# Left-over channels of two projections as half-height matmuls in alternating rows

## What is computed

```python
Qs = (msa[:, :, 0] @ Wq_s) * scale_s              # query of row 0, per column
sw = softmax(Qs @ Ks)                             # over the 128 rows, Ks = msa @ Wk_s
Q = (x @ Wq) * scaling * sw
K = x @ Wk
V = x @ Wv
QK = einsum('brihd,brjhd->bhij', Q, K)            # 192 x 192 per head, summed over rows
out = einsum('bhij,brjhd->brihd', softmax(QK), V)
x = x + out
```

## Time and profile before

| | us |
|---|---|
| three runs | 669.31, 673.8, 676.18 |
| median | 673.8 |
| span of the profiled execution | 670.4 |
| TensorE matmul busy | 521.5 |
| TensorE weight loads busy (beside matmuls) | 427.5 |
| VectorE busy | 436.3 |
| ScalarE busy | 253.9 |
| GpSimd busy | 225.4 |

### The profile page before, as it was taken

How to read it: one execution, slowest core, us unless ns; L and a number is a source line. 1 busy time by engine, 2 the same in 40 slices (tenths; PEclk the granted TensorE clock), 3 DMA queues, 4 the chain that set the end, 5 groups by cost and what they waited for, 6 DMA issues and landing times.

```text
span 670.4 us, 14214 instructions
## 1 busy us (share of the span) xinstructions
PE 521.5 (78%) x4984; PEld 427.5 (64%) x4984; DVE 436.3 (65%) x981; ACT 253.9 (38%) x555; POOL 225.4 (34%) x231
## 2 busy tenths in 40 slices
PE   0040499997279999999989999999799999157771
PEld 0030288987246666666659999999799888146561
DVE  3999757899726666666664668777556794224453
ACT  0030255786135565556550216555311233022221
POOL 1010123688013333333330005665400084134444
PEclk9995565998579999999999999999899999587887
DMA  8991015789937677777856006777379999999997
GB/s 285 421 427 68 0 48 142 221 237 250 241 107 267 225 246 245 228 265 222 259 153 225 1 15 221 236 237 235 122 251 336 315 315 321 313 315 293 307 285 216
DMA packets 122265, 152.81 MB, mean 228 GB/s; under 512 B 21552, under 2 KB 107120, under 8 KB 120432
## 3 DMA queue, kind: packets, MB, share of 16 engines
q1 hardware_dynamic: 119968, 151.01, 71.3%
q10 hardware_dynamic: 2256, 1.23, 0.7%
HBM read 95.60 MB, written 56.62 MB: 227 GB/s over the span
## 4 chain that ended last, share of the span: by engine, by line
PE 61%; SPq 12%; DVE 11%; DMA 9%; POOL 2%; issue 2%; ACTq 1%; ACT 1%; POOLq 0%; DVEq 0%
DMA BIG<-in_x 7%; PE PS L978 7%; PE PS L979 7%; PE PS L980 7%; PE PS L981 7%; PE PS L982 7%; DVE EXTRA L591 6%; PE PS L1010 4%; PE PS L860 3%; PE PS L1039 3%; PE PS L1040 2%; PE PS L1043 2%; PE PS L1041 2%; PE PS L1042 2%; SPq L422 2%; SPq L397 2%
## 5 line engine op out<-in xcount | busy, mean ns | idle before, releaser
L457 POOL TENSOR_TENSOR BIG<-EXTRA,BIG 128x192 f32 (+1 forms) x144 | 106.5, 740 | 208.5 <-ACT BIG L529 208.3
L758 DVE TENSOR_TENSOR EXTRA<-PS,SW 128x192 f32<-128x192 f32 (+1 forms) x144 | 73.4, 510 | 81.7 <-ACT BIG L542 81.7
L978 PE MATMUL PS<-WP,EXTRA 128*128 128x384 f16 (+1 forms) x384 | 110.4, 288 | 14.2 <-DMA EXTRA<-xt_scratch 12.9
L979 PE MATMUL PS<-WP,EXTRA 128*128 128x384 f16 (+1 forms) x384 | 110.4, 288 | 0.0
L980 PE MATMUL PS<-WP,EXTRA 128*128 128x384 f16 (+1 forms) x384 | 110.4, 288 | 0.0
L981 PE MATMUL PS<-WP,EXTRA 128*128 128x384 f16 (+1 forms) x384 | 110.3, 287 | 0.0
L982 PE MATMUL PS<-WP,EXTRA 128*128 128x384 f16 (+1 forms) x384 | 110.2, 287 | 0.0
L827 DVE SCALAR_TENSOR_TENSOR BIG<-PS,small,BIG 128x512 f32<-128x512 f32 x96 | 64.5, 736 | 60.5 <-DMA BIG<-in_x 57.4
L467 POOL TENSOR_TENSOR BIG<-BIG,EXTRA 64x512 f32<-64x512 f32 x48 | 60.3, 1256 | 119.7 <-DVE BIG L827 62.6
L1010 PE MATMUL PS<-BIG,EXTRA 128*128 128x256 f16 x576 | 69.4, 286 | 31.7 <-DVE BIG L827 31.7
L1010 PEld LDWEIGHTS PS<-BIG,EXTRA 128*128 128x128 f16 x576 | 58.8, 103 | 42.0 <-DVE BIG L827 32.8
(11 more groups left out here) (157 smaller groups left out, 958.2 us busy)
## 6 DMA issues: line engine op xcount, KB each, us to landing
EXTRA<-xt_scratch SPq DMA_DIRECT2D x48, 512.0 KB, 3.6
BIG<-in_x SPq DMA_DIRECT2D x6, 3072.0 KB, 20.9
v_scratch<-EXTRA SPq DMA_DIRECT2D x48, 384.0 KB, 3.8
EXTRA<-xt_scratch SPq DMA_DIRECT2D x48, 256.0 KB, 3.8
BIG<-in_x SPq DMA_DIRECT2D x8, 1536.0 KB, 13.1
out_x<-BIG SPq DMA_DIRECT2D x8, 1536.0 KB, 12.8
BIG<-v_scratch SPq DMA_DIRECT2D x6, 1536.0 KB, 10.9
xt_scratch<-BIG SPq DMA_DIRECT2D x12, 512.0 KB, 3.3
```

The lines of the kernel that those rows point to most:

```text
L457: pool.tensor_tensor(QA[:, :, bass.ds(SI[h] * n + low, SI[h])], TQ[h][g % 4], QA[:, :, bass.ds(SI[h] * n, SI[h])], ALU.subtract).then_inc( ...
L758: v.tensor_tensor(TQ[h][g % 4].rearrange("p (m d) i -> p m d i", d=D), ps[:, :, 0:EH].rearrange("p i (m d) -> p m d i", d=D), swv.unsqueez ...
L978: mm(po, xh0, WP[:, 0, 0, wc], start=True, stop=False)
L979: mm(po, xh0, WP[:, 1, 0, wc], start=False, stop=False)
```

## The change

The left-over 64 channels are stored as pairs of columns: an even column in rows 0 to 63 and the odd column next to it in rows 64 to 127, highs and lows in different slots. A pair of columns is then projected by six matmuls of 128 rows (three for each column, as before) and six of 64 rows (x highs with weight highs, x highs with weight lows, x lows with weight highs; for the even column in the upper rows, then for the odd one in the lower rows, in turn). The product of x lows with weight lows, which L982 included, is no longer made. The stores to DRAM go from seven to five DMAs for two chunks. For h = 1 the two columns of a pair lie in different PSUM banks, so KA is read with one more dimension (ScalarE and VectorE), and q's multiplication is made in two instructions of two columns.

```diff
-        STORES = 16 * 7
+        STORES = 16 * 5
...
-            return ps if h == 0 else ps.rearrange("p a (b n) -> p (a b) n", b=2)
+            return ps if h == 0 else ps.rearrange("p a (b n) -> p b a n", b=2)
...
-                for s in range(2):
-                    to = rest[s * E1:(s + 1) * E1]
-                    sp.dma_start(to[:, :, 0, :], mixed[0:E1, s::2, :]).then_inc(stored, 16)
-                    sp.dma_start(to[:, :, 1, :], odd[E1:P, s::2, :]).then_inc(stored, 16)
+                sp.dma_start(rest[0:E1], mixed[0:E1]).then_inc(stored, 16)
+                sp.dma_start(rest[E1:P], odd[E1:P]).then_inc(stored, 16)
...
-                        nc.scalar.copy(KA[:, :, bass.ds(SI[h] * n, SI[h])],
-                                       ps[:, :, EH:2 * EH].rearrange("p i m -> p m i")).then_inc(s_kvh[h], 1)
+                        if h == 0:
...
+                        else:
+                            nc.scalar.copy(KA[:, :, bass.ds(SI[h] * n, SI[h])].rearrange("p m (b a) -> p m b a", a=2),
+                                           ps[:, :, :, EH:2 * EH].rearrange("p b a m -> p m b a")
+                                           ).then_inc(s_kvh[h], 1)
...
-                        v.tensor_tensor(TQ[h][g % 4].rearrange("p (m d) i -> p m d i", d=D),
-                                        ps[:, :, 0:EH].rearrange("p i (m d) -> p m d i", d=D),
-                                        swv.unsqueeze(2).to_broadcast([P, HALF, D, si]),
-                                        ALU.mult).then_inc(s_tq[h], 1)
+                        tq = TQ[h][g % 4].rearrange("p (m d) i -> p m d i", d=D)
+                        for i in range(0, si, 2):
+                            pq = ps[:, :, 0:EH] if h == 0 else ps[:, i // 2, :, 0:EH]
+                            ins = v.tensor_tensor(tq[:, :, :, i:i + 2], pq.rearrange("p i (m d) -> p m d i", d=D),
+                                                  swv[:, :, i:i + 2].unsqueeze(2).to_broadcast([P, HALF, D, 2]),
+                                                  ALU.mult)
+                        ins.then_inc(s_tq[h], 1)
...
-                    for i in range(SI[h]):
-                        il = at + i
-                        po = ps[:, i, 0:CW[h]]
-                        slot = (il % 2) * (CI // 2) + il // 2
-                        xh0 = XT[b][:, slot * R:(slot + 1) * R]
-                        xl0 = XT[b][:, (CI + slot) * R:(CI + slot + 1) * R]
-                        x1 = XT[b][:, (2 * CI + slot) * R:(2 * CI + slot + 1) * R]
-                        mm(po, xh0, WP[:, 0, 0, wc], start=True, stop=False)
-                        mm(po, xh0, WP[:, 1, 0, wc], start=False, stop=False)
-                        mm(po, xl0, WP[:, 0, 0, wc], start=False, stop=False)
-                        mm(po, x1, WP[:, 0, 1, wc], start=False, stop=False)
-                        ins = mm(po, x1, WP[:, 1, 1, wc], start=False, stop=True)
+                    for even in range(0, SI[h], 2):
+                        outs = [ps[:, i, 0:CW[h]] if h == 0 else ps[:, even // 2, i, 0:CW[h]] for i in range(2)]
+                        for i in range(2):
+                            il = at + even + i
+                            po = outs[i]
+                            slot = (il % 2) * (CI // 2) + il // 2
+                            xh0 = XT[b][:, slot * R:(slot + 1) * R]
+                            xl0 = XT[b][:, (CI + slot) * R:(CI + slot + 1) * R]
+                            mm(po, xh0, WP[:, 0, 0, wc], start=even == 0, stop=False, skip_group_check=True)
+                            mm(po, xh0, WP[:, 1, 0, wc], start=False, stop=False, skip_group_check=True)
+                            mm(po, xl0, WP[:, 0, 0, wc], start=False, stop=False, skip_group_check=True)
+
+                        for s, w in ((0, 0), (0, 1), (1, 0)):
+                            for i, rows in ((0, slice(0, E1)), (1, slice(E1, P))):
+                                o = (2 * CI + s * (CI // 2) + (at + even) // 2) * R
+                                ins = mm(outs[i], XT[b][rows, o:o + R], WP[rows, w, 1, wc],
+                                         start=False, stop=s == 1, skip_group_check=True)
```

More of the change, by code:

```diff
@@ L320, in _ @@
                 full = xt_dram[c // 2, :, 0:4 * CI * R].rearrange("p (c a n) -> p c a n", a=2, n=512)
-                rest = xt_dram[c // 2, :, 4 * CI * R:6 * CI * R].rearrange("p (c a n) -> p c a n", a=2, n=512)
+                rest = xt_dram[c // 2, :, 4 * CI * R:6 * CI * R].rearrange("p (c n) -> p c n", n=512)
                 src = BIG[:, c * CI * E:(c + 2) * CI * E].bitcast(fp16)
@@ L541, in body @@
                                            ps[:, :, 2 * EH:2 * EH + E]).then_inc(s_kvh[h], 1)
-                        nc.scalar.copy(KA[:, :, bass.ds(SI[h] * n, SI[h])],
-                                       ps[:, :, EH:2 * EH].rearrange("p i m -> p m i")).then_inc(s_kvh[h], 1)
+                        if h == 0:
+                            nc.scalar.copy(KA[:, :, bass.ds(SI[h] * n, SI[h])],
+                                           ps[:, :, EH:2 * EH].rearrange("p i m -> p m i")).then_inc(s_kvh[h], 1)
+                        else:
+                            nc.scalar.copy(KA[:, :, bass.ds(SI[h] * n, SI[h])].rearrange("p m (b a) -> p m b a", a=2),
+                                           ps[:, :, :, EH:2 * EH].rearrange("p b a m -> p m b a")
+                                           ).then_inc(s_kvh[h], 1)
                         if g or not isinstance(t, int):
@@ L765, in body @@
                                             ALU.subtract)
-                        v.tensor_tensor(KA[:, :, bass.ds(si * n + C, si)],
-                                        ps[:, :, EH:2 * EH].rearrange("p i m -> p m i"),
-                                        KA[:, :, bass.ds(si * n, si)], ALU.subtract).then_inc(s_kvl[h], 1)
+                        kl, kh = (KA[:, :, bass.ds(si * n + o, si)] for o in (C, 0))
+                        if h == 0:
+                            pk = ps[:, :, EH:2 * EH].rearrange("p i m -> p m i")
+                        else:
+                            pk = ps[:, :, :, EH:2 * EH].rearrange("p b a m -> p m b a")
+                            kl, kh = (q.rearrange("p m (b a) -> p m b a", a=2) for q in (kl, kh))
+                        v.tensor_tensor(kl, pk, kh, ALU.subtract).then_inc(s_kvl[h], 1)
                 body(0)
```

## The result

The changed kernel takes 686.15 us (683.09 to 686.99, 4 runs) against 674.99 us of the kernel before (669.31 to 677.97, 4 runs): a ratio of 1.018 (95% interval 1.012 to 1.023). The forecast was 688.8 us, 15.0 us over the kernel before; it came out 11.2 us over.

The account below looks back on a forecast made before the run. TensorE was taken to bound the projections, with SP's stores setting their start. Span 670.4 + 20.0 (matmuls and switches) − 5 (stores) = 685.4 us; the median, 673.8 + 15.0, gives 688.8 us, range 664 to 722.

Parts of the forecast that it names:

- The bound: Projection stages: TensorE is busy all the time, so time added to a step's TensorE work shows in full.
- The overlap: Projection matmuls: upper and lower halves run together, six taking the time of three; 23.5 us back in all.
- The stagger: Half-height matmuls: the second of an upper and lower pair needs its own weights first, 17 ns once a pair.
- The change of height: Projection steps: each switch between 128 and 64 rows costs 105 ns (90 + 15), two switches a pair.
- The sum of the two: Both projection halves, switches and stagger less the saved matmul: +6.1 us and +13.9 us, +20.0 us together.
- The stores: SP's queue before the projections: five DMAs for seven, 5.8 to 6.0 us a pair of chunks, saving 5 us.
- VectorE at nothing: Projection steps: split q multiplication and reordered KA reads cost nothing, hidden behind the TensorE step.
- A: Rival at the projection matmuls: no overlap, halves run one after the other, 67.4 us more, 756 us; chance 0.14.
- B: Rival at the height switches: the switch is free, its drain hidden, so the kernel is faster, 648.5 us; chance 0.13.
- C: Rival at the stores: the whole 12.9 us wait before the projections goes, 680.9 us; chance 0.11.
- the break-even: Height switches in the projections: below 66 ns a switch the change wins.
- the 15 ns between an upper and a lower start: Sign in the projection timeline: an upper and a lower matmul start some 15 ns apart.

Follow-up runs that it names:

- run 3: Changed kernel with three full-height matmuls in place of a pair's six half-height ones, so no change of height (products not the reference's): 644.53 us, ratio 0.958.
- run 8: Kernel before with only q's second-half multiplication split into two instructions of 192 elements: 675.18 us against 673.44, ratio 1.0039.
- run 6: Changed kernel with all six half-height matmuls of a pair in rows 0 to 63: 845.36 us.
- run 1: Changed kernel with a pair's half-height matmuls ordered three upper, then three lower, instead of in turn: 687.08 us, ratio 1.024 to the kernel before.

## Why the prediction was right

**The bound.** TensorE sets the step, and no other engine or transfer took over, down to 1.46 and 0.74 us a pair (run 3). Shown.

**The overlap.** Forecast at its full bound, and it is there; the gain of one matmul a pair is real. The stagger was booked at 17 ns and is within 4: a pair takes 1.675 and 0.955 us where the forecast's terms give 1.69 and 0.97. The Trainium skill's 4 ns ("TensorE: Matmul & The Clock Gate", Part 3) fits the trace: two together span 0.34 us where one spans 0.33.

**The change of height.** Forecast 105 ns, from fp32 rows; measured 106 to 107 ns in fp16, in four kernels with changes against the one without. Its two pieces hold too, 0.09 us of pause and 0.01 to 0.02 us for the exposed load. This is the term that made the sign of the result, and it could be read from four transposes of the kernel before. The Trainium skill, "TensorEngine Tiling (Array Packing)", Key Properties, says that a change of the tiling mode drains TensorE. The trace agrees for fp16 now as well, with 0.09 us of pause.

**The sum of the two.** +20.0 us forecast; by the measured periods 96 x (0.050 + 0.130) = 17.3 us. The difference is nearly all the stagger, 2 x 96 x 13 ns = 2.5 us. In the two profiles the projection stages grew by 3.8 + 12.2 = 16.0 us; the 1.3 us between that and the periods, in the first half above all, are not accounted for.

**The stores.** 5 us forecast, with 5.8 to 6.0 us a pair of chunks; measured 5.8 us a pair, and a start 5.3 us earlier by the means of twelve profiles. That the transfers then set the pace fits the DMA share of 0.95; no run varied the bytes. The later landing of the reload was not in my sum, and the shorter run of the stores made up for it: that the two cancel is luck. In the changed kernel's own profile the start moved by 2.8 us only. Its third pair of stores began at 120.33 us in place of 118.35, which is spread: with five stores that point lies anywhere between 117.9 and 120.4.

**VectorE at nothing.** Right, if the 0.4% of run 8 is no effect. The reordered reads of KA had no run of their own, but run 3 has them, and the split too, and its pair takes nine matmul times.

**Rivals.** A was ruled out by the timeline, and run 6 made it on purpose: it costs 159 us over the changed kernel, over twice the 67 that I gave it: I had given a fall of the clock no more than the tail of this rival, and it made some 90 of the 159 us. B (a free change) is out: 106 ns, not under 66. But the break-even that it rested on was the useful number, since it says what a better order has to reach. C is out: 7.9 of the 12.9 us wait are still there, and no profile starts the projections before 181.4 us.

**Wrong steps beside it.** Of what was to show the forecast, the 15 ns between an upper and a lower start did not come; they are within 4 ns. And in run 1 I expected matmuls to start strictly in program order. It shows that half-height matmuls in other rows don't wait for those in front of them in the program.

## What to carry to other kernels

Count the places where the number of active rows changes before counting the matmuls saved: each costs 106 ns here, more than a matmul of 192 columns. Half-height matmuls pay when they are put in long blocks, and mirroring the order of neighbouring steps at least halves the changes at no price in buffers: the same products went from 686 to 662 us so, and with blocks over two steps to 651, past the 672 us of the kernel before. And look for a rare line of the old kernel that does what the new one will do often.

## What the runs showed of the hardware that I had not expected

- Three half-height matmuls in the upper rows followed by three in the lower rows take as long as in turn (0.67 and 0.66 us for six): the lower rows' work starts beside the upper rows' work that stands before it in the program.
- With all half-height matmuls in the same rows, the granted clock stayed at 0.50 through a stage of some 190 us in which the records show TensorE busy (10.00 of 10.00 us from 460 to 470). In the first half, with 384 columns in place of 192, it rose from 0.50 to 1.00 under the same sequence.
- One VectorE multiplication of 384 elements took 813 ns, and two of 192 elements, which do the same work, 0.62 us together (run 8). Which operand's pattern makes the long one slow was not tried.
